# Half of the expert items moved into the causal attention, on one pair of score banks, with all loops unrolled

## The reference, cut to what matters

```python
# block 1: causal attention, 16 heads of 8, inside each of the 16 rows
att = where(causal, einsum('bhqd,bhkd->bhqk', q, k) * hd**-0.5, big_neg)
x1  = softmax(att) @ v ; x1 = x1 @ W_proj          # weights scaled by spectral norm
# block 2: 8 experts, the best two of the gate; H = 512
mask = softmax(where(gate >= kth, gate, -inf))
h = relu(einsum('bsd,edh->bseh', x, W1) + b1)
y = (einsum('bseh,ehd->bsed', h, W2) + b2) * mask ; mean over the experts
# block 3: attention over the 16 batch rows at each position, with a position
# term (cumulated sigmoid gates, interpolated between position logits)
attn_logits += cope(q, attn_logits, pos_emb) ; softmax ; @ v ; @ Wo
# block 4: feed-forward 128 -> 64 -> 64 x 16 -> 64 -> 128
```

## Time and profile before

| | us |
|---|---|
| median of 3 runs | 3000.72 |
| lowest, highest | 2977.73, 3016.37 |
| profiled execution, its own time | 2990.51 |
| span of its trace | 2988.8 |
| granted clock, mean | 0.831 |
| busy: PE, PEld, DVE, ACT, POOL | 2380.3, 1366.5, 1848.0, 1131.0, 800.3 |
| instructions in the span | 47082 |

### The profile page before, as it was taken

The page is one execution under the profiler, slowest core; times in us unless marked ns, Lnnn a source line. Parts: engine busy times, 40 slices in busy tenths (PEclk is TensorE's granted clock), DMA queues, the critical chain, the costliest instruction groups (busy, mean ns, idle before and its releaser), DMA issues.

```text
span 2988.8 us, 47082 instructions
## 1 busy us (share of the span) xinstructions
PE 2380.3 (80%) x13325; PEld 1366.5 (46%) x13325; DVE 1848.0 (62%) x3363; ACT 1131.0 (38%) x2437; POOL 800.3 (27%) x1462
## 2 busy tenths in 40 slices
PE   3888888888888978999889898989898988744443
PEld 1233333333333225666566566656665666522222
DVE  4455555555555420111777787788778877888884
ACT  0344444444444422333333443344344433322222
POOL 3233333333333211222322323222322232111110
PEclk7788778887888658999999899989998999866666
DMA  5432222322223001000000000000000000000000
GB/s 136 100 66 45 44 49 54 73 45 44 45 55 74 4 1 49 37 28 29 29 2 31 32 28 4 32 32 28 4 32 32 28 4 32 4 0 4 4 4 7
DMA packets 87793, 100.90 MB, mean 34 GB/s; under 512 B 11065, under 2 KB 82369, under 8 KB 83521
## 3 DMA queue, kind: packets, MB, share of 16 engines
q1 hardware_dynamic: 80770, 94.42, 12.9%
q10 hardware_dynamic: 6848, 4.36, 0.5%
HBM read 68.35 MB, written 29.62 MB: 33 GB/s over the span
## 4 chain that ended last, share of the span: by engine, by line
PE 20%; DVE 17%; issue 6%; POOL 4%; ACT 3%; DVEq 1%; ACTq 0%; POOLq 0%
PE rest_bank L967 6%; PE rest_bank L953 6%; DVE logits L1156 3%; DVE prod L1154 3%; PE rest_bank L1023 3%; DVE acc L1195 2%; POOL rstd2b L1430 2%; POOL rstd2b L1428 1%; DVE stats2b L1081 1%; ACT y L1340 1%; PE rest_bank L989 1%; PE rest_bank L961 1%; PE rest_bank L975 1%; PE rest_bank L998 1%; DVE mv2b L1084 1%
## 5 line engine op out<-in xcount | busy, mean ns | idle before, releaser
L967 PEld LDWEIGHTS rest_bank<-w,hidden 128*128 128x128 f32 x4096 | 558.9, 200 | 239.0 <-issue 234.1
L456 DVE TENSOR_REDUCE maxima<-scores 128x2 f32<-128x1024 f32 (+3 forms) x512 | 416.0, 822 | 402.1 <-PE scores L345 401.5
L953 PE MATMUL rest_bank<-xe,w 128*128 128x512 f32 x1024 | 560.2, 634 | 91.5 <-ACT hidden L1415 77.0
L967 PE MATMUL rest_bank<-w,hidden 128*128 128x128 f32 x4096 | 562.8, 283 | 0.0
L1415 ACT ACTIVATE hidden<-rest_bank 128x512 f32<-128x512 f32 x512 | 303.6, 595 | 631.6 <-PE rest_bank L953 492.2
L545 ACT ACTIVATE probs<-turned 128x512 f32<-128x512 f32 (+3 forms) x1024 | 396.2, 439 | 331.3 <-PE turned L363 277.4
L363 PE MATMUL turned<-q_stack,k_stack 51*128 51x512 bf16 (+3 forms) x1024 | 262.5, 360 | 150.2 <-DMA q_stack<-max_rows 85.3
L614 POOL TENSOR_SCALAR_AFFINE_SELECT probs<-probs 128x256 f32<-128x256 f32 x512 | 209.1, 410 | 618.9 <-ACT probs L545 618.6
L1443 POOL TENSOR_TENSOR xe<-xn_t,mask_all 128x512 f32<-128x512 f32 x128 | 176.6, 1391 | 472.4 <-ACT xn_t L1352 356.6
L953 PEld LDWEIGHTS rest_bank<-xe,w 128*128 128x128 f32 x1024 | 177.4, 200 | 185.0 <-issue 92.8
L374 PE MATMUL o_bank<-probs,v_ext 128*32 128x512 f32 (+3 forms) x2048 | 242.4, 553 | 0.2 <-POOL probs L614 0.2
(11 more groups left out here) (203 smaller groups left out, 2997.3 us busy)
## 6 DMA issues: line engine op xcount, KB each, us to landing
mask_all<-mask_scratch SPq DMA_DIRECT2D x32, 1024.0 KB, 5.5
stack_q<-parts_q SPq DMA_DIRECT2D x96, 128.0 KB, 2.4
stack_k<-parts_k SPq DMA_DIRECT2D x96, 128.0 KB, 2.4
q_stack<-stack_q SPq DMA_DIRECT2D x32, 384.0 KB, 5.8
k_stack<-stack_k SPq DMA_DIRECT2D x32, 384.0 KB, 10.1
x<-in_L_attn_batch_dram SPq DMA_DIRECT2D x16, 256.0 KB, 5.3
w<-in_L_ffn_W_dram ACTq DMA_DIRECT2D x16, 256.0 KB, 3.1
out_dram<-x SPq DMA_DIRECT2D x16, 256.0 KB, 2.3
```

What stands on the lines that cost most here:

```text
L456: dve.tensor_reduce(mx[:, w % 2, :, p, qt], s_bank[s % 2][:, :, 0:(qt + 1) * P], AX.X, ALU.max)\
L953: pe.matmul(h_bank[k % 2][:, :], t.w1[:, k // F, (k % F) * P:(k % F + 1) * P], xe[:, k // F % XE, :], start=True, stop=True).then_inc(s_h, 1)
L967: mm = pe.matmul(y_bank[:, j * P:(j + 1) * P], hidden[:, k % 4, j * P:(j + 1) * P], t.w2[:, k, :], start=False, stop=(k == E * F - 1), ski ...
```

## The change

- Expert groups are cut anew: groups 0 to 7 are the batch rows 0 to 7 (their 4 chunks), groups 8 to 15 the other half of each chunk. Their helpers move into a new function `experts`, which both parts use.
- The items of groups 0 to 7 (256 of 512) run inside `causal_attention`, from batch row 3 on, in 5 of each 8 steps (0, 2, 3, 5, 7): 20 a row. The product of an item stands in the next step, ahead of the next hidden matmul. Gates, mask and sum of those groups are put into slots of the batch rows; the mask DMAs between the maxima rows on SP.
- PSUM in the attention: one pair of score banks where two were, and the two banks that come free are one hidden bank and one sum bank. `v_maxima` now stands first in DVE's step.
- Scratch is shared: `rest` and `xn` lie in `attn_t`, `y` in `xn1`, with waits for it.
- The folding of the bias into w1 goes into batch row 1, one expert every 4 steps, through the hidden bank.
- The second part: 20 steps instead of 22. Two with 32 items (groups 8, 9), one with 16, then 11 with 16 items (in every second slot) beside attention, six without; gates and sums in alternate ones. Keys and values of group i + 3 stand in attending step i, while there are any.
- Every loop over rows or steps is unrolled.

The core of the diff:

```diff
+FIRST_ITEM_ROW, HIDDEN_AT = 3, (0, 2, 3, 5, 7)
+ROW_GROUPS = 8
+ROW_ITEMS = 4 * E * ROW_GROUPS
+GATES_IN_ROW = {2: 0, 3: 1, 5: 2, 6: 3, 8: 4, 9: 5, 11: 6, 13: 7, 15: 8}
+HIGH_AFTER = {(2, 3): 0, (4, 2): 1, (5, 0): 2, (7, 2): 3, (9, 1): 4, (10, 3): 5, (12, 1): 6, (13, 0): 7, (15, 3): 8}
...
+    def first_tile(j):
+        return S * ((j - ROW_GROUPS) // 2) + R * (2 + (j - ROW_GROUPS) % 2)
+
+    def block(j):
+
+        return x_t[:, :, j, :] if j < ROW_GROUPS else t.x[:, first_tile(j):first_tile(j) + G, :]
...
+    def pe_columns(pe, e, bank):
+        if e == 0:
+            pe.wait_ge(t.experts_loaded, 32 * E)
+            pe.wait_ge(m.s_means, 2)
+            pe.wait_ge(m.s_b1, 16)
+        else:
+            pe.wait_ge(m.s_biased, e)
+        pe.matmul(bank[:, :], minus_mean, t.w1[:, e, :], start=True, stop=False)
+        pe.matmul(bank[:, :], plus_mean, b1_row[:, e, :], start=False, stop=True).then_inc(m.s_columns, 1)
+
+    def v_biased_weights(dve, e, bank):
+        dve.wait_ge(m.s_columns, e + 1)
+        dve.tensor_tensor(t.w1[:, e, :], t.w1[:, e, :], bank[:, :], ALU.add).then_inc(m.s_biased, 1)
...
+    def d_mask_low(sp, j, s_read, value):
+        await_(sp, passed["sync"], s_read, value)
+        if j > 0:
+            await_(sp, passed["sync"], m.s_mask_lo, 16 * j)
+            await_(sp, passed["sync"], m.s_mask_hi, 16 * j)
+        sp.dma_start(mask_scratch, m.mask_t[:, :]).then_inc(m.s_mask_out, 16)
+        if j > 0:
+            await_(sp, passed["sync"], m.s_xe, E * j - 4)
+        else:
+            await_(sp, passed["sync"], m.s_biased, E)
+        await_(sp, passed["sync"], m.s_mask_out, 16 * j + 16)
+        sp.dma_start(m.mask_all[:, 0:E // 2, :], mask_from[:, 0:E // 2, :]).then_inc(m.s_mask_lo, 16)
+
+    def d_mask_high(sp, j):
+        if j > 0:
+            await_(sp, passed["sync"], m.s_xe, E * j)
+        sp.dma_start(m.mask_all[:, E // 2:E, :], mask_from[:, E // 2:E, :]).then_inc(m.s_mask_hi, 16)
...
+    def p_weighted_rows(pool, x):
+
+        j, e = x // E, x % E
+        if e == 0:
+            await_(pool, passed["pool"], m.s_mask_lo, 16 * j + 16)
+            await_(pool, passed["pool"], m.s_xt, j + 1)
+        if e == E // 2:
+            await_(pool, passed["pool"], m.s_mask_hi, 16 * j + 16)
+        if x >= XE:
+            await_(pool, passed["pool"], m.s_h, F * (x - XE + 1))
+        pool.tensor_tensor(m.xe[:, x % XE, :], m.xn1_t[:, :], m.mask_all[:, e, :], ALU.mult).then_inc(m.s_xe, 1)
...
+    def pe_hidden(pe, q, bank, freed):
+        x, f = q // F, q % F
+        if f == 0:
+            pe.wait_ge(m.s_xe, x + 1)
+        if q == 0:
+            pe.wait_ge(m.s_biased, E)
+        if freed > 0:
+            pe.wait_ge(m.s_relu, freed)
+        pe.matmul(bank[:, :], t.w1[:, x % E, f * P:(f + 1) * P], m.xe[:, x % XE, :], start=True, stop=True).then_inc(m.s_h, 1)
+
+    def a_relu(act, q, bank):
+        if q >= 4:
+            act.wait_ge(m.s_y, q - 3)
+        await_(act, passed["scalar"], m.s_h, q + 1)
+        act.activation(m.hidden[:, q % 4, :], bank[:, :], ACT.Relu).then_inc(m.s_relu, 1)
+
+    def pe_expert(pe, q, bank):
+        j, k = q // (E * F), q % (E * F)
+        if k == 0:
+            if j > 0:
+                pe.wait_ge(m.s_total, j)
+            for n in range(G):
+                pe.matmul(bank[:, n * P:(n + 1) * P], m.mask_t[:, n * P:(n + 1) * P], t.b2[:, :],
+                          start=(n == 0), stop=False, skip_group_check=True)
+        pe.wait_ge(m.s_relu, q + 1)
+        for n in range(G):
+            mm = pe.matmul(bank[:, n * P:(n + 1) * P], m.hidden[:, q % 4, n * P:(n + 1) * P], t.w2[:, k, :],
+                           start=False, stop=(k == E * F - 1), skip_group_check=True)
+        mm.then_inc(m.s_y, 1)
...
+    def a_total(act, j, bank):
+        if j > 0:
+            await_(act, passed["scalar"], m.s_x1, j)
+        await_(act, passed["scalar"], m.s_y, E * F * (j + 1))
+        act.activation(m.total[:, :, :], bank[:, :].rearrange("p (g d) -> p g d", g=G), ACT.Copy).then_inc(m.s_total, 1)
...
+def item_at(b, w, s):
+
+    if b < FIRST_ITEM_ROW or s not in HIDDEN_AT:
+        return None
+    return len(HIDDEN_AT) * (QUADS * (b - FIRST_ITEM_ROW) + w) + HIDDEN_AT.index(s)
...
-        s_bank = [ctx.enter_context(nc.psum_tensor(f"scores{i}", [P, 2, 512], F32)) for i in range(2)]
+        s_bank = ctx.enter_context(nc.psum_tensor("scores", [P, 2, 512], F32))
...
+        h_bank = ctx.enter_context(nc.psum_tensor("hidden_bank", [P, 512], F32))
+        y_bank = ctx.enter_context(nc.psum_tensor("experts_bank", [P, 512], F32))
...
+        rest, xn = attn_t, attn_t[:, :].rearrange("p (c d) -> p c d", d=D)
+        xn_t, y = sb("xn_t", [P, N]), m.xn1
...
-            pe.wait_ge(s_tile_max, 32 * b + 8 * w + s + 1)
+            if 32 * b + 8 * w + s > 0:
+                pe.wait_ge(s_tile_max, 32 * b + 8 * w + s)
...
+                    if gates is not None and w == 0 and s == 7:
+                        pe_fill_wait(pe, fill_no(b, "rows_turned"))
+                        m.pe_turn_rows(pe, gates, misc, s_misc)
+                    if gates is not None and w == 1 and s == 0:
+                        pe_fill_wait(pe, fill_no(b, "gates"))
+                        m.pe_gates(pe, misc, s_misc)
+                    if gates is not None and w == 1 and s == 7:
+                        pe_fill_wait(pe, fill_no(b, "mask"))
+                        m.pe_mask(pe, gates, misc, s_misc)
+                    if b == 1 and s in (0, 4):
+                        m.pe_columns(pe, 2 * w + s // 4, h_bank)
+                    before, item = item_at(*step_before(b, w, s)), item_at(b, w, s)
+                    if before is not None and before < ROW_ITEMS:
+                        m.pe_expert(pe, before, y_bank)
+                    if item is not None and item < ROW_ITEMS:
+                        m.pe_hidden(pe, item, h_bank, item)
...
+                    if b == 1 and s in (1, 5):
+                        m.v_biased_weights(dve, 2 * w + s // 4, h_bank)
+                    if gates is not None and w == 0 and s == 2:
+                        m.v_row_stats(dve, gates)
+                    if gates is not None and w == 1 and s == 0:
+                        m.v_gates(dve, gates, misc, s_misc, fill_no(b, "gates") + 1, s_misc_read)
+                    if gates is not None and w == 1 and s == 4:
+                        m.v_mask(dve, gates)
+                    item = item_at(b, w, s)
+                    if item is not None and item >= E * F and item % (E * F) == 1:
+                        m.v_sum_stats(dve, item // (E * F) - 1)
+                    if item is not None and item >= E * F and item % (E * F) == 3:
+                        m.v_sum_add(dve, item // (E * F) - 1)
...
+                    if gates is not None and w == 0 and s == 4:
+                        m.a_rows(act, gates)
+                    if gates is not None and w == 0 and s == 7:
+                        a_copy_misc(act, m.xn1_t2[:, :], fill_no(b, "rows_turned"))
+                    if gates is not None and w == 1 and s == 2:
+                        m.a_gate_exp(act, gates)
+                    if gates is not None and w == 1 and s == 7:
+                        m.a_mask(act, misc, s_misc, fill_no(b, "mask") + 1, s_misc_read)
+                    if gates == 0 and w == 2 and s == 0:
+                        m.a_expert_rows(act, 0)
+                    item = item_at(b, w, s)
+                    if item is not None and item >= E * F and item % (E * F) == 0:
+                        m.a_total(act, item // (E * F) - 1, y_bank)
+                    if item is not None and item >= E * F and item % (E * F) == 2:
+                        m.a_sum_scale(act, item // (E * F) - 1)
+                    if item is not None and item % (E * F) == 22:
+                        m.a_expert_rows(act, item // (E * F) + 1)
+                    if item is not None and item < ROW_ITEMS:
+                        m.a_relu(act, item, h_bank)
...
+                    if gates is not None and w == 0 and s == 3:
+                        m.p_row_root(pool, gates)
+                    if gates == 0 and w == 3 and s in (2, 4):
+                        m.p_weighted_rows(pool, s // 2 - 1)
+                    item = item_at(b, w, s)
+                    if item is not None and item >= E * F and item % (E * F) == 1:
+                        m.p_sum_root(pool, item // (E * F) - 1)
+                    if item is not None and item % F == 0 and item // F + 2 < E * ROW_GROUPS:
+                        m.p_weighted_rows(pool, item // F + 2)
...
+            for w in range(1, QUADS):
+                d_max_rows(sp, par, w, fill_no(b, f"max{w}"))
+                if w == 2 and b in GATES_IN_ROW:
+                    m.d_mask_low(sp, GATES_IN_ROW[b], s_misc_read, fill_no(b, "mask") + 2)
+                if (b, w) in HIGH_AFTER:
+                    m.d_mask_high(sp, HIGH_AFTER[b, w])
...
+def all_steps():
```

(33 more changed lines are left out.)

925 lines of the change are left out of this document (447 added, 478 removed).

## The result

The kernel before runs at 2992.8 us (median of 19 runs, 2974.7 to 3025.7), the changed one at 3010.1 us (19 runs, 2985.9 to 3015.3): a ratio of 1.0048, 95% interval 1.0027 to 1.0069. It is slower by half a per cent, within 2% of the kernel before. The forecast was 3038 us, that is +47 on the profiled execution; the profiled executions differ by 19.5 us (spans 2988.8 and 3008.3), the medians by 17.3.

The account below looks back on a forecast made before the run. PE was taken to bound the causal attention, with gaps, and PE with DVE hardly less the mixed steps. Rows 3 to 15 +270, rows 0 to 2 +35 and second stage -258 gave +47 on 2990.5: 3038 us, range 2925 to 3150.

Parts of the forecast that it names:

- Rival 1: Both stages: packing works better, rows at 76 us and steps at 88, total 2902 us; chance 0.2.
- rival 2: Rows 3 to 15: row stays wait-bound or clock near 0.8, row 92 us, total 3165 us; chance 0.3.
- rival 3: Second stage: half items don't relieve it, steps stay at 97 us, total 3093 us; chance 0.12.
- 1.5 for the weighted rows' use of the port: Ten second-stage steps with 16 items: 1.5 us added to each, as POOL's weighted rows contend with DVE.
- PE's stream: A row of 3 to 15: attention 39.4 us, 20 items 35.0, gates and other small matmuls 1.9.
- The new waits: Rows 3 to 15: waits from the single hidden bank and single score pair, 1.6 us a quad, 6.5 a row.
- The waits of 118 us: Rows 3 to 15: PE's waits before the turned products, 64 us of them for the maxima rows' DMA, would go.
- a sign of being wrong: Before hidden matmuls: a wait for a mask DMA or POOL's weighted rows, counted at nothing, would make the prediction wrong.
- The assumption called the weakest: Rows 3 to 15: granted clock near full, over 0.9, where it was 0.78.
- The bound of 92: Upper bound of a row of 3 to 15: today's waits stay, 62.2 + 35 less five us.
- The pair: Batch rows 0 to 2: single pair of score banks makes scores wait for the maximum, 1.4 us a quad, +12 us.
- the columns and gates: Batch rows 0 to 2: weight columns in row 1, gates of row 2 and the expert weights' wait, +23 us.

Follow-up runs that it names:

- experiment 3: Changed kernel with the matmuls of the 256 items in batch rows 3 to 15 cut to 64 (hidden) and 16 (product) columns: 3313.9 us.
- experiment 4: Kernel before with one pair of score banks, plus five 128x512 matmuls a quad that nothing reads in batch rows 1 to 15: 3118.8 us.
- experiment 5: Changed kernel with 12 items a batch row instead of 20, experts and gates of batch rows 4 to 7 left out: 2822.9 us.
- experiment 1: Kernel before with one pair of score banks instead of two and nothing else of the change: 3127.6 us.
- experiment 7: Changed kernel with a second pair of score banks until the items begin: 2995.4 us.
- experiment 6: Changed kernel with the keys' chain of the second stage a few slots earlier: 2970.9 us.
- experiment 10: Experiment 9's version with the last addition of a second-stage step moved into the next step: 2855.7 us.
- experiment 11: Experiment 10's version with the first kv addition behind the second product of weights and values: 2823.3 us.
- experiment 9: Changed kernel with 12 items a batch row, second-stage steps of 24, a second score pair until items begin, and an earlier keys' chain: 2893.4 us.

## Why the prediction's sum was wrong, and what of its mechanism held

The direction held, and the mechanism of the forecast: a large cost in the rows, a nearly equal gain in the second stage. Rival 1 (rows below 78 or steps below 88) and rival 2 (row at 92, over 88, or a clock near 0.8) fell by the row of 82.0 at clock 1.00, rival 3 (steps at 97) by the step of 90.2. But the size was wrong: +19.5 was measured for +47. The sum is a small difference of two large terms, and 23 us too little gain in the second stage and 12 us too much cost in rows 3 to 15, against 8 us too little in rows 0 to 2, make up these 27. The step that failed is the sizing of the second stage, above all of its ten steps with half items, taken at 91.5 us each and measured at 90.2.

**The second stage, -281 for -258, is the step that was mis-sized most.** From the end of the attention, 1392.4: the fill and two pure steps 133.1 for 139, the half step and the first attending one 113.2 for 116, the ten steps 902.4 for 915, the tail 467.2 for 468. So more than half is the 91.5 a step. It was the 90.1 of the step without experts plus 1.5 for the weighted rows' use of the port, gates and sum costing about the same. Measured are 91.2 with gates and 89.7 with a sum, and DVE is busy 75.0 where 77 was forecast. The 1.5 that the prediction adds to every step is, on DVE, 2.0 in the four steps with gates and nothing in the others:

```profile
1901.47 0.29 DVE L1451 TENSOR_TENSOR acc<-acc,prod 128x128 f32<-128x128 f32 x1
1901.80 0.23 DVE L1451 TENSOR_TENSOR acc<-acc,logits 128x64 f32<-128x64 f32 x1
...
1985.51 7.61 POOL L445 TENSOR_TENSOR xe<-xn_t,mask_all 128x512 f32<-128x512 f32 x2 [18.97 <-ACT xn_t L433]
...
1990.64 1.35 DVE L1451 TENSOR_TENSOR acc<-acc,prod 128x128 f32<-128x128 f32 x1
1992.03 1.18 DVE L1451 TENSOR_TENSOR acc<-acc,logits 128x64 f32<-128x64 f32 x1
```

In the four steps with gates two of POOL's weighted rows fall beside DVE's additions. The first takes 6.0 to 6.3 us (to 1991.85 here), and DVE's last two additions take 1.35 and 1.18 where they take 0.29 and 0.23 in the step ahead of it, in which no weighted row stands there. The kernel before has this in each of its mixed steps. POOL's other rows of these ten steps, 33 of 37, last 1.3 us, as those in the batch rows do, so the moved rows do meet no one, as the prediction had it. A step with 16 items and a sum costs no more than the old one with a sum and no items. So in the ten steps this cost DVE 8 us and not the 15 of the forecast, which is 7 of the 13 by which they were counted too long. Where the other 6 come from, and why the work ahead of them was 9 us shorter than counted, no run tells apart: these causes stay open. Against steps as the kernel before has them when written out (98.8), the half items bring 9 us; unrolling brings another 1.8 a step. The forecast had unrolling at nothing. Its steps were built on the straight step of 90.1, so they were not wrong by it, but the account of what the change brings was: in the kernel before it alone is worth 24 us, most of them in these steps.

**Rows 3 to 15, 82.0 for 83.** This is nearly right because errors offset. PE's stream, 39.4 + 35.0 + 1.9 = 76.3, measured 78.4 of busy time a row. An item takes about 2.0 us of it and not 1.75, by its starts:

```profile
893.29 1.16 PE L474 MATMUL experts_bank<-w,hidden 128*128 128x128 f32 x8 [0.17 <-ACT hidden L462]
894.28 1.02 PE L456 MATMUL hidden_bank<-xe,w 128*128 128x512 f32 x2
895.24 0.39 PE L649 MATMUL turned<-q_stack,k_stack 51*128 51x512 bf16 x2
```

That is 0.99 + 0.96; over all rows the items take 39.7 a row instead of 35.0, and all other work 38.6 instead of 41.3 (some of this may be only a shift from a record to its neighbour, but the sum is not). The new waits, put at 6.5, are 3.7 of idle time in all: 1.7 for the relu, 0.8 for the maxima, 0.9 for DVE's outputs, 0.3 for the exponentials. The waits of 118 us went as forecast, and no mask DMA and no weighted row stands before a hidden matmul there. In the second stage POOL's weighted rows are waited for before hidden matmuls, which the prediction counted at nothing in the steps and had named as a sign of being wrong: 7.6 us once at its start, where 5 were put for the fill, and 6.5 in all in four of the steps, each time behind one of the long rows.

The assumption called the weakest, the clock near full, was right, and it is what carries the result. Experiments 3, 4 and 5 show how much hangs on it: 20 added matmuls a row, some 22 us, are free at 0.97, and rows with thinned items take 106.8 at 0.54. The bound of 92 ("the waits of today stay") had counted the items on top of a slow row; nothing in the runs comes near it as long as the items are whole.

**Rows 0 to 2, 42.6 for 35, but for other reasons.** The pair was put at +12, at most 17, and the columns and gates at +23. The pair alone costs 34.9 (experiment 1). The count by starts missed the 14 scores ahead of row 0, where PE has nothing else, and put the rest at 12 where it is 24.7. Given back beside columns and gates the pair brings 12 (experiment 7). The two costs do not add; that each fills the other's waits is a reading and was not measured apart. And the 12 of experiment 7 agrees with the forecast's 12 by luck: the forecast had them in the twelve quads of rows 0 to 2, measured they lie before the first copy, where it had nothing, and behind it the pair brings nothing in sum. The advice to double-buffer in the Trainium skill, page "Trainium Kernel Development and Optimization", section "Best Practices", which the prediction cites, stands there for overlapping DMA with compute; for banks between two engines experiments 1 and 7 have the price here.

**The same holds for the whole row.** The single pair costs 6.6 a row by itself, 1.65 a quad where 1.4 was counted. Beside 20 items it costs 0.8. But it was needed to free the banks of the items, so the change's 19.8 a row can be put, in this order, as 6.6 for the pair and 13.2 for 20 items, and the last eight of these account for all of the 13.2.

**What the change got wrong** follows: it moves 20 items into a row, eight more than the row takes for nothing, and empties a stage in which PE then idles a third of the time and DVE sets the step. At the margin an item costs 1.70 us in a row; in the steps, from 16 to 24 items, (91.2 - 87.9) / 8 = 0.4.

## What to carry to other kernels

A forecast that is the difference of two large terms is as uncertain as both together: here errors of 5% and 9% in two terms of some 260 us each made a sum of +47 come out at +19.5. Before moving work between stages, price it at the margin in both: how much each stage takes for nothing, and what the next piece costs there. Full-width matmuls placed into a wait-bound stretch of PE may pay for themselves by the granted clock, and thinning them may cost more than it saves; look at the clock beside the busy share. Where one engine sets the step and is still idle a sixth of it, follow each of its waits back and start that chain earlier, or put other work ahead of it: here that brought 39, 38 and 32 us (experiments 6, 10 and 11), more in sum than taking eight items from each row into the steps (66, experiment 9).
